# The turning of Y: from TensorE transposes to 32x32 squares on VectorE and four DMAs

## The reference

```
xz = xn @ in_proj_w.T;  x_branch, z = split(xz)          # 1024 each
x_branch = silu(causal_conv(x_branch, 4 taps) + conv_b)
proj = x_branch @ x_proj_w.T  ->  X (16 heads x 64), dt, B, C (128 each)
dt = softplus(dt @ dt_proj_w.T + dt_proj_b);  A = -exp(A_log)
Y = ssd(X * dt, A * dt, B, C) + X * D
attn = (Y * silu(z)) @ out_proj_w.T
ffn  = (sigmoid(xn @ q(w1).T) * (xn @ q(w2).T)) @ q(w3).T   # q: weights rounded to -1, 0, 1
```

## Time and profile before

| | |
|---|---|
| median of 3 runs | 1686.59 us (1686.47 to 1687.39) |
| the profiled execution: its own time / its span | 1687.1 us / 1685.2 us |
| mean granted TensorE clock | 0.981 |
| PE busy | 1599.0 us, 95% of the span |
| DVE / ACT / POOL busy | 1129.8 (67%) / 913.9 (54%) / 487.2 us (29%) |
| DMA queue of SP | 46960 packets, 88.08 MB, 16.4% of 16 engines |
| chain that ended last, by engine | PE 77%, DVE 9%, ACT 7%, issue 5%, DMA 2% |

### The profile page before, as it was taken

The page is one execution under the profiler, slowest core; times in us unless marked ns, Lnnn a source line. Parts: engine busy times, 40 slices in busy tenths (PEclk is TensorE's granted clock), DMA queues, the critical chain, the costliest instruction groups (busy, mean ns, idle before and its releaser), DMA issues.

```text
span 1685.2 us, 25445 instructions
## 1 busy us (share of the span) xinstructions
PE 1599.0 (95%) x9426; PEld 783.6 (47%) x9426; DVE 1129.8 (67%) x1826; ACT 913.9 (54%) x1871; POOL 487.2 (29%) x469
## 2 busy tenths in 40 slices
PE   6487879999999999999999999999999999999999
PEld 3233334445444544444444454444544544444444
DVE  6766876687556875667756776568855687566762
ACT  6676545566355653556444763556636565356641
POOL 4223212144131440324212441213403233033320
PEclk9798999999999999999999999999999999999999
DMA  6344330112001110011101110011100121002200
GB/s 224 113 158 143 101 113 20 43 53 57 26 7 58 51 45 19 26 58 45 51 1 38 58 58 26 7 46 63 39 26 14 53 62 51 1 26 67 54 7 26
DMA packets 47084, 89.71 MB, mean 53 GB/s; under 512 B 5968, under 2 KB 6736, under 8 KB 46960
## 3 DMA queue, kind: packets, MB, share of 16 engines
q1 hardware_dynamic: 46960, 88.08, 16.4%
HBM read 79.41 MB, written 8.65 MB: 52 GB/s over the span
## 4 chain that ended last, share of the span: by engine, by line
PE 77%; DVE 9%; ACT 7%; issue 5%; DMA 2%; POOL 0%; SPq 0%; DVEq 0%; ACTq 0%; POOLq 0%
PE bank L560 18%; PE bank L472 13%; PE bank L576 9%; PE bank L385 9%; PE bank L401 8%; PE bank L542 7%; PE bank L411 5%; ACT edc L785 3%; PE bank L504 2%; PE bank L516 2%; PE bank L489 1%; PE bank L532 1%; DVE edc L1119 1%; DMA arena<-w_in 1%; DVE mdc L1125 1%
## 5 line engine op out<-in xcount | busy, mean ns | idle before, releaser
L472 PE MATMUL bank<-wx_hi,arena 128*128 128x512 f16 x1024 | 321.2, 384 | 0.0
L560 PE MATMUL bank<-xt_hi,q 128*128 128x512 f16 x704 | 266.8, 379 | 1.2 <-ACT q L847 1.2
L560 PE MATMUL bank<-xt_lo,q 128*128 128x512 f16 x704 | 266.8, 379 | 0.0
L1381 POOL TENSOR_TENSOR xst<-xdt,dst 128x512 f32<-128x512 f32 x64 | 66.7, 1042 | 571.5 <-DVE xdt L1073 571.5
L472 PE MATMUL bank<-wx_lo,arena 128*128 128x512 f16 x512 | 196.6, 384 | 0.0
L576 PE MATMUL bank<-q,arena 128*128 128x512 fp8e4 x704 | 162.4, 379 | 0.0
L785 ACT ACTIVATE edc<-csl,csv 128x128 f32<-128x128 f32 x512 | 155.8, 389 | 0.0
L472 PEld LDWEIGHTS bank<-wx_hi,arena 128*128 128x128 f16 x1024 | 101.4, 99 | 115.8 <-issue 6.2
L1119 DVE TENSOR_TENSOR edc<-edc,gt 128x512 f32<-128x512 f32 x128 | 87.9, 727 | 66.3 <-ACT edc L790 66.3
L815 ACT CAST arena<-full 128x512 f16<-128x512 f32 x88 | 54.6, 620 | 137.9 <-DVE full L1174 137.9
L1174 DVE SCALAR_TENSOR_TENSOR full<-tnh,bank 128x512 f32<-128x512 f32 x88 | 60.4, 687 | 100.7 <-PE bank L560 100.7
(11 more groups left out here) (184 smaller groups left out, 3523.8 us busy)
## 6 DMA issues: line engine op xcount, KB each, us to landing
csl<-sums SPq DMA_DIRECT2D x128, 256.0 KB, 3.2
res<-w_ffn SPq DMA_DIRECT2D x41, 256.0 KB, 3.7
res<-x SPq DMA_DIRECT2D x32, 256.0 KB, 3.9
out<-res SPq DMA_DIRECT2D x32, 256.0 KB, 2.0
arena<-w_x SPq DMA_DIRECT2D x8, 640.0 KB, 4.7
yac<-x SPq DMA_DIRECT2D x16, 256.0 KB, 2.7
gate<-x SPq DMA_DIRECT2D x16, 256.0 KB, 3.4
arena<-w_in SPq DMA_DIRECT2D x8, 512.0 KB, 6.4
```

Source lines behind the costliest of these rows:

```text
L472: i = pe.matmul(banks[0][:], act[:, k, c * P:(c + 1) * P], wt[:, k, hf * half:(hf + 1) * half], start=(n == 1), stop=(n == 3 * ki))
L560: i = pe.matmul(banks[2 * (m % 2) + j][:], q12[:, j, k, m * P:(m + 1) * P], part[:, k, :], start=(n == 1), stop=(n == 2 * kd))
L1381: pool.tensor_tensor(by_head(xst[:], hd), by_head(xdt[:], hd), heads_over(sml["dst"][:, c, :], hf * hph, hph, hd), ALU.mult).then_inc(S["x ...
```

## The change

- **Gate.** The multiply of Y by the gate goes from DVE to POOL, behind POOL's addition, with a wait for `y_added` and `gate`.
- **Squares.** DVE transposes each 32x32 square of `yac` by itself (one instruction, `turn_y`, behind `xdt_lo`) into `xs[u % 2]`.
- **DRAM.** ACT writes this tile to `y_dram` with one DMA (`write_y`) and, at the unit's end, reads it back with four DMAs (`read_y`), one per 32 partitions, whose pieces are 32 elements long: the squares land in the places that make the whole transpose. They land in `yac[u % 2]` (units 6 and 7: in `xs`). `read_y` waits for the write of the same unit.
- **Split.** `split_y(u-1)` on ACT and DVE takes the high and low part from this tile in SBUF instead of from bank 7, late in unit u; those of unit 7 go into step 4 of the FFN.
- **Output projection.** PE's `turn_y` is gone. `project_out` is done by halves: 12 products for unit u-2 in each of units 2 to 7, the last two behind FFN steps 2 and 6. DVE adds the bank to `res` in units 3, 5 and 7 and in FFN step 7.
- **Moved buffers and waits.** The ring of four FFN weight tiles uses `csl` in place of `xs`; the scales product of block 0 uses bank 3 in place of bank 7; the waits that protected `yac`, `xs` and bank 7 follow the new readers.

```diff
-              "diag_mm": 16, "st_mm": 8, "y_turned": 8, "out_mm": 4, "up_mm": 22, "down_mm": 4,
+              "diag_mm": 16, "st_mm": 8, "out_mm": 8, "up_mm": 22, "down_mm": 4,
...
+        ysq = [xs[u % 2] for u in range(len(units))]
+        yf = [yac[u % 2] if u < 6 else xs[u % 2] for u in range(len(units))]
+        y_dram = nc.dram_tensor("y_squares", [halves, P, half], F32, kind="Internal").ap()
...
-        ffn_ring = [edc[0], edc[1], xs[0], xs[1]]
+        ffn_ring = [edc[0], edc[1], csl[0], csl[1]]
...
+        def squares(dram, j):
+
+            return dram.rearrange("(i a) (k j b) -> j a k i b", a=SQ, b=SQ, j=P // SQ)[j]
+
+        def by_feature(t, j):
+            return t[j * SQ:(j + 1) * SQ, :].rearrange("a (k i b) -> a k i b", i=P // SQ, b=SQ)
...
-            def turn_y(b, u):
...
-            def project_out(b, j):
-                pe.wait_ge(S["yt_lo"], at(b, "yt_lo", 2 * j + 1))
+                pe.wait_ge(S["yt_lo"], at(b, "yt_lo", u))
                 n = 0
-                for k in range(ki):
+                for k in range(hf * per, (hf + 1) * per):
                     for act, wt in passes(yt, wo):
...
-                    if u and u % 2 == 0:
-                        project_out(b, u // 2 - 1)
+                    if u >= 2:
+                        project_out(b, u - 2)
...
-                    if m == 0:
-                        turn_y(b, 7)
-                    if m == 1:
-                        project_out(b, 3)
+                    if m in (2, 6):
+                        project_out(b, 6 if m == 2 else 7)
...
+            def write_y(b, u):
+                hf, n = u % 2, chunks * b + u // 2
+                act.wait_ge(S["y_blocks"], at(b, "y_blocks", u))
+                if n:
+
+                    act.wait_ge(D[f"y_in{hf}"], n * (P // SQ) * DMA)
+                act.dma_start(y_dram[hf], ysq[u][:]).then_inc(D[f"y_out{hf}"], DMA)
+
+            def read_y(b, u):
+                hf, n = u % 2, chunks * b + u // 2
+                act.wait_ge(D[f"y_out{hf}"], (n + 1) * DMA)
+                for j in range(P // SQ):
+                    act.dma_start(by_feature(yf[u], j), squares(y_dram[hf], j)).then_inc(
+                        D[f"y_in{hf}"], DMA)
...
-                    if u:
-                        turn_y(b, u - 1)
...
+                    write_y(b, u)
+                    if u:
+                        split_y(b, u - 1)
                     if u + 2 < len(units):
                         project_z(b, u + 2)
                     split_state(b, u)
+                    read_y(b, u)
...
-                dve.wait_ge(S["y_added"], at(b, "y_added", u))
-                dve.tensor_tensor(y_[:], y_[:], gate[u % 2][:], ALU.mult).then_inc(S["y_gated"], 1)
 
             def turn_y(b, u):
+                dve.wait_ge(S["y_gated"], at(b, "y_gated", u))
+                dve.transpose(ysq[u][:], yac[u % 2][:]).then_inc(S["y_blocks"], 1)
...
+                pool.wait_ge(S["y_added"], at(b, "y_added", u))
+                pool.wait_ge(S["gate"], at(b, "gate", u))
+                pool.tensor_tensor(yac[u % 2][:], yac[u % 2][:], gate[u % 2][:],
+                                   ALU.mult).then_inc(S["y_gated"], 1)
```

More of the change, by code:

```diff
@@ L110, in mamba_ffn_block @@
               *(f"early{n}" for n in range(4)), *(f"late{n}" for n in range(3)),
-              *(f"beside{n}" for n in range(4)), "sums_out", "sums_in0", "sums_in1")}
+              *(f"beside{n}" for n in range(4)), "sums_out", "sums_in0", "sums_in1",
+             "y_out0", "y_out1", "y_in0", "y_in1")}
         def sb(name, shape, dt=F32):
@@ L518, in update, with project_out @@
                 i.then_inc(S["st_mm"], 1)
-            def turn_y(b, u):
-                if u % 2:
-                    pe.wait_ge(S["yt_lo"], at(b, "yt_lo", u - 1))
-                elif u:
-                    pe.wait_ge(S["attn"], at(b, "attn", u // 2 - 1))
[L525 to L534, removed]
-            def project_out(b, j):
-                pe.wait_ge(S["yt_lo"], at(b, "yt_lo", 2 * j + 1))
+            def project_out(b, u):
+                hf = u % 2
+                if u == 0:
+                    pe.wait_ge(S["acc"], at(b, "acc", 7))
+                elif hf == 0:
+                    pe.wait_ge(S["attn"], at(b, "attn", u // 2 - 1))
+                pe.wait_ge(S["yt_lo"], at(b, "yt_lo", u))
                 n = 0
-                for k in range(ki):
+                for k in range(hf * per, (hf + 1) * per):
                     for act, wt in passes(yt, wo):
@@ L542, in project_out @@
                         i = pe.matmul(banks[7][:], act[:, k, :], wt[:, k, :],
-                                      start=(n == 1), stop=(n == 3 * ki))
+                                      start=(hf == 0 and n == 1), stop=(hf == 1 and n == 3 * per))
                 i.then_inc(S["out_mm"], 1)
@@ L551, in ffn_up @@
                         pe.wait_ge(S["hid_f"], at(b, "hid_f", m - 2))
+                    elif m == 1 and j == 1 and b == 0:
+                        pe.wait_ge(S["gam"], 1)
                     elif m == 0 and j == 0:
@@ L746, in project_x @@
                 if u >= 2:
-                    act.wait_ge(S["y_skip"], at(b, "y_skip", u - 2))
+                    act.wait_ge(D[f"y_out{u % 2}"], (chunks * b + u // 2) * DMA)
                 else:
@@ L937, in scalar_program @@
                         aside()
-                    if m == 0:
-                        turn_y(b, 7)
+                    if m == 4:
+                        split_y(b, 7)
                 if b < nb - 1:
@@ L1313, in vector_program @@
                     split_state(b, u)
+                    if u >= 3 and u % 2:
+                        project_out(b, u // 2 - 1)
                 for m in range(kf):
```

51 lines of the change are left out of this document (26 added, 25 removed).

## The result

| | before | after |
|---|---|---|
| median | 1686.89 us (4 runs) | 1849.16 us (4 runs) |
| ratio, 95% interval | | 1.097 [1.0957, 1.0983] |
| profiled execution / span | 1687.1 / 1685.2 us | 1851.1 / 1849.3 us |
| mean granted TensorE clock | 0.981 | 0.946 |

Slower by 162 us; forecast were 90, and the range of the forecast ended at 1850, which is where the change came out (1.097 times 1686.59 is 1850.2).

The account below looks back on a forecast made before the run. TensorE bounded the kernel before; after the change the ACT/DVE loop (13.7 us against TensorE's 11.5) would. 1687.1 + 79 (seven blocks) + 4 (block 0) + 7 (clock) = 1777 us, range 1700 to 1850.

Parts of the forecast that it names:

- The forecast case: ACT/DVE loop in units 1 to 6 bounds at 13.7 us against TensorE's 11.5; 1777 us, chance 0.47.
- read_y: four DMAs ... 0.33 + 3 x 0.43 = 1.6: Loop term: four read issues hold ACT's queue 1.6 us before the next relu; bounds 0 and 3.9.
- rival 1: Dear issues: 512 pieces hold ACT's sequencer 0.7 to 0.97 us each; 1827 to 1874 us; chance 0.17 with rival 2.
- Y landing late: Rival 2: reads need over 12 us, split_y waits on ACT; each further us costs 42; chance 0.17 with rival 1.
- A store of 256 KB lands 2.0 us after its issue: Loop term: write_y, issued at 3.0 us after xdt_hi, lands at 5.0.
- The end of the units and the FFN: FFN begins 8.8 us after xdt_hi(7), plus 1 us a block for the slow clock, 7 in all.
- Block 0: First block, bound by preparation on ACT and DVE: +4 us, between -5 and +15.
- DVE stands still beside POOL: In the loop, xdt_lo waits for POOL's 1.28 us gate multiply, ends at 1.85; xst_hi starts at 2.95.
- rival 3: POOL's multiply holds nobody up: loop 13.0 us, +5.15 us a block, 1727 us; chance 0.20.
- The rule on ports: VectorE and GpSimd share one SBUF port pair, locked a whole instruction by whoever starts first; with it 1777, without it rival 3.
- rival 4: Issues cost nothing; ACT's sequencer pushes DMAs while activations run: loop 12.1 us, 1703 us, or 1658 without DVE's standstill; chance 0.16.
- TensorE's gain: Removing 64 groups of four transposes saves TensorE 3.5 us a block; with waits 4.4, at most 31 us over seven blocks.

Follow-up runs that it names:

- Run 6: The changed kernel with each of the four reads of Y as 32 whole rows of 2 KB, not 512 pieces of 128 bytes: 1801.53 us, 1.0679.
- Run 1: The changed kernel with the gate multiply back on DVE, the rest of the change kept: 1866.72 us, 1.1081 against the kernel before.
- run 3: The changed kernel with SP instead of ACT issuing the write and reads of Y in blocks 1 to 7: 1735.61 us, 1.03.
- run 7: Run 4 without DVE's transpose of the squares, the write taking yac itself: 1702.76 us, 1.0097.
- run 4: Run 3 (SP issues the write and reads of Y) with the gate multiply on DVE: 1733.37 us, 1.0284.
- run 2: The changed kernel with ACT's four reads of Y moved later in its queue, into the next unit between xs and xdt_hi: 1733.87 us, 1.029.
- run 12: Control: the kernel before with FFN steps 0 and 1 moved into units 2 and 7, unit 7's turning and last output projection two steps later: 1677.29 us, 0.9948.
- run 14: Run 4 plus late block 0 reads, early FFN steps, later unit 6 output product, sooner x loads, block 0's unit 7 Y read behind FFN step 1: 1666.54 us, 0.9888.

## Why the prediction was wrong

- **What bounds.** The forecast case is the one that came: ACT's and DVE's loop bounds in units 1 to 6, the units end late, the slow clock adds to it. The relu follows xdt_hi by 7.45 us (6.7 forecast). The size failed: 162 us against 90. Of the 74 us that the profiled execution lies above 1777, the short loop is 25, the long loops 24, block 0 17 and the rest 8.
- **The step that failed most is the term "read_y: four DMAs ... 0.33 + 3 x 0.43 = 1.6".** The four took 2.67: 0.66 each, near the lower end of rival 1 (0.7 to 0.97), to which I had given 0.17 together with Y landing late. (Y was in time: the reads landed 2.2 to 6.2 us after their issue.) Run 6 splits the price: 0.44 for whole rows as for SP's, 0.22 for 512 pieces. With the 0.4 that the rest of the loop was shorter, the short loop of 14.3 is worth 3.6 us a block.
- **Long loops were not in the sum.** "A store of 256 KB lands 2.0 us after its issue" held for 23 of the 42 writes in the loops of blocks 1 to 7; the other 19 took 2.2 to 3.9 and cost some 17 us together. In 6 loops one issue took 1.3 to 1.7 us, 5 us more. This makes the mean 14.88 and is worth another 3.5 us a block. The packets show what stands beside them. Two writes of the change from issue to landing, a long one (1322.13 to 1325.74) and below it a short one (1307.83 to 1309.84; queue and kind: packets, MB, share of the 16 engines; then count, KB, us to landing):

```profile
q8 instruction: 1, 0.02, 2.7%
y_squares<-xs ACTq DMA_DIRECT2D x1, 256.0 KB, 3.6
```

```profile
y_squares<-xs ACTq DMA_DIRECT2D x1, 256.0 KB, 2.0
```

The long one has a packet of the kind "instruction", 16 KB that take 1.5 us; the short one has none. All 19 long writes have such a packet (of 16 or 8 KB) between issue and landing, and 3 of the 23 others; all 6 long issues have one of 16 KB beside them, and 4 of the 162 others. Runs 1 and 6 read the same way (18 and 17 long writes, each with its packet). That the loading of instructions makes them long is argued from this, not shown: no run varied it. I had asked how long a write takes once, not how often it takes longer in 42 loops without slack.
- **The end of the units and the FFN.** From xdt_hi(7) to the FFN 9.65 us stand against 8.8 + 1 of the forecast. The sum is right, its terms are not: the twelve products at the lower clock cost 2.3 us more in block 1 and 0.7 to 2.3 in the seven blocks, 1.5 on average and not 1, and the rest is shorter by as much. Behind the start of the FFN 110.48 stand against 108.98 in blocks 1 to 6: ACT's four issues of unit 7 are ahead of the first tanh, for which TensorE waits 8.0 us in six blocks. With SP's issues (run 3) the stretch is 108.98.
- **Block 0.** Taken +4, bounded at +15, found +21.0: 12.7 ahead of its FFN and 8.3 behind its start. Late reads gave back 13.2 of it (block 1's first xdt_hi from 361.17 to 348.02), leaving the transpose out gave 4.7 (run 7), and reading the Y of unit 7 behind FFN step 1 gave 3.7 us of the time. Neither the transpose nor the FFN of block 0 had a term there.
- **DVE stands still beside POOL.** The step holds in its mechanism: xdt_lo ends 0.55 us after POOL's operation beside it, before (351.56, 352.11) and after (371.86, 372.41). But POOL's multiply starts at 370.21, 0.55 us ahead of xdt_hi and not with it, so xdt_lo ends 1.65 us behind the start of xdt_hi, as before (1.64), and not 1.85; what comes later is xst_hi (2.58, before 1.13), behind POOL. POOL's two products beside it take 1574 and 1383 ns on average (before, one of 1042), which the sum had at 1.28 and 1.04 us. Its price did not hold: I had put 50 us between the forecast and rival 3. Run 1, which takes POOL's multiply away, lets the write go 0.35 us sooner and loses 18 us in all; the multiply's 0.72 on DVE weigh more.
- **The rule on ports** (the Trainium skill, "SBUF — State Buffer", "SBUF: two separate sides") agrees with more rows than I had used. yt_lo with both sources in SBUF takes 1525 ns in the 42 cases where POOL works beside it and 687 in the 22 where it does not; from the bank it takes 679 beside POOL and 687 without. And m_mult is stretched in runs 3 and 4. I applied it to the operation that moved, not to those whose neighbours it moved.
- **Issues cost nothing** (rival 4). Not at this place; at another place (run 2) they do. The Trainium skill's page "DMA: Bandwidth & Descriptors", section "Issuing engines are not separate DMA queues", calls the sequencer's time usually small beside the DMA. That fits a DMA alone, 0.66 of 2.5 us; it says nothing of an engine that computes behind it.
- **TensorE's gain is real.** 3.5 us a block of TensorE's work were forecast for the transposes; 3.1 are seen between runs 12 and 14, of which 1.9 come out as time. To get it, five causes of waiting had to be taken away one after another: ACT's issues, the short units, the tanh of step 0, DVE's sum of chunk 2 and the load of x.

## What to carry to other kernels

A DMA on an engine that computes is an instruction with a price in that engine's order, more for many small pieces; put it where the engine waits anyway, and look up what stands behind it on the new queue. When a loop has about 1 us of slack, add up every row of both engines, also the one that "waits anyway": its cover goes when the loop is mended. Count a DMA in such a loop by how long it takes on average, not at best. When work leaves the bounding engine, fill the hole from elsewhere in the program: the change as it stood lost 9.7%, with its issues moved and the holes filled it gains 1.1%, of which the filling alone gives 0.5%.

## What was not expected of the hardware

- An issue on ACT's queue: 0.33 us for one write of 128 rows of 2 KB, 0.44 in a row of reads of whole rows, 0.66 with 512 pieces of 128 bytes, up to 1.72. On SP's queue the same reads take 0.64.
- ACT's sequencer issues while an activation runs (the write at 373.40, xst_hi from 373.34 to 373.97), and the activation listed behind the issues starts when they end (the reads to 378.11, the relu at 378.21).
- DVE's pass over two SBUF tensors took 1525 ns beside POOL and 687 alone; with one source in a bank it took 679 beside POOL.
- Each of the 19 writes that landed late had a packet of instructions between its issue and its landing.
- The clock was 0.51 in the 10.4 us from 458.90 on, which begin inside a wait of 4.4 us, and 1.00 from 234.57 to 1664.76 in run 14, where no wait of TensorE from block 1 on is over 1 us.
